# A two-level routing index, shorter last norms, reordered last sums and a gate in halves in a fused decoder layer

## What is computed

```python
x = _layernorm(x + attn(x))                # 32 heads of 8, relative bias, softmax
x = _layernorm(x + xattn(ctx_1024, x))     # state scan over 256 tokens, 16 states, gated by silu(x)
x = _layernorm(x + ffn(x))                 # 4 experts, top 1: y_e(x) * softmax weight
```

```python
logits = x @ Wr + br
probs = softmax(logits)
top_w, top_idx = top_k(probs, 1)
h = silu(x @ Wg[e]) * (x @ Wu[e]);  y = h @ Wd[e];  out = y[top_idx] * top_w
```

## Time and profile before

| what | value |
|---|---|
| median of three runs | 485.94 us |
| the profiled execution | 486.2 us |
| its span, first to last instruction | 484.5 us |
| mean granted TensorE clock | 0.958 of full speed |
| busy: PE, PEld | 427.5 us (88%), 215.6 us (45%) |
| busy: DVE, POOL, ACT | 316.5 us, 224.7 us, 210.1 us |
| DMA | 49.37 MB, mean 102 GB/s |

### The profile page before, as it was taken

How to read it: one execution, slowest core, us unless ns; L and a number is a source line. 1 busy time by engine, 2 the same in 40 slices (tenths; PEclk the granted TensorE clock), 3 DMA queues, 4 the chain that set the end, 5 groups by cost and what they waited for, 6 DMA issues and landing times.

```text
span 484.5 us, 8012 instructions
## 1 busy us (share of the span) xinstructions
PE 427.5 (88%) x2643; PEld 215.6 (45%) x2644; DVE 316.5 (65%) x620; ACT 210.1 (43%) x410; POOL 224.7 (46%) x246
## 2 busy tenths in 40 slices
PE   5889698868788998989989999876899999999993
PEld 3445123323234443444434443454446666666652
DVE  3598568999987888868888776588113334433344
ACT  2556446657554556745766458311011222111120
POOL 2000518787786679967799589300541111111001
PEclk9999766999989999999999999989799999999998
DMA  8789939527254282744345320198110000000000
GB/s 234 106 261 96 336 101 113 110 99 99 87 100 100 79 118 88 135 152 197 132 156 147 115 87 1 37 361 254 50 38 11 12 4 8 11 11 11 11 2 8
DMA packets 39366, 49.37 MB, mean 102 GB/s; under 512 B 4664, under 2 KB 32673, under 8 KB 39334
## 3 DMA queue, kind: packets, MB, share of 16 engines
q1 hardware_dynamic: 36322, 46.65, 37.8%
q0 software_dynamic: 1056, 2.10, 1.4%
q10 hardware_dynamic: 1956, 0.21, 0.4%
HBM read 40.72 MB, written 8.91 MB: 102 GB/s over the span
## 4 chain that ended last, share of the span: by engine, by line
PE 61%; DVE 20%; issue 7%; POOL 7%; ACT 2%; DMA 2%; POOLq 0%; SPq 0%; DVEq 0%
PE ps L1144 16%; PE ps L1160 8%; PE ps L870 7%; PE ps L897 5%; DVE arena L1532 5%; PE ps L901 4%; PE ps L943 4%; DVE arena L1465 4%; PE ps L770 3%; DVE arena L1483 3%; POOL arena L641 2%; PE ps L930 2%; PE ps L1152 2%; POOL arena L647 2%; PE ps L783 1%
## 5 line engine op out<-in xcount | busy, mean ns | idle before, releaser
L1336 ACT ACTIVATE arena<-ps 128x512 f32<-128x512 f32 x128 | 76.2, 595 | 90.7 <-PE ps L930 90.5
L1483 DVE TENSOR_REDUCE arena<-ps 128x2 f32<-128x512 f32 x128 | 86.3, 681 | 27.4 <-PE ps L901 23.3
L647 POOL TENSOR_TENSOR arena<-arena 128x512 f32<-128x512 f32 x60 | 76.3, 1272 | 41.6 <-DVE arena L1532 41.5
L641 POOL TENSOR_TENSOR arena<-arena 128x512 f32<-128x512 f32 x64 | 87.1, 1363 | 4.2 <-issue 4.0
L1144 PE MATMUL ps<-arena 128*128 x176 | 77.5, 593 | 0.6 <-ACT arena L1373 0.6
L1532 DVE TENSOR_TENSOR_SCAN arena<-ps,arena 128x512 f32<-128x512 f32 x60 | 72.8, 1214 | 0.5 <-DVE mv L1577 0.2
L870 PE MATMUL ps<-arena,identf 128*128 128x512 f32 x128 | 68.5, 625 | 0.0
L897 PE MATMUL ps<-arena 48*128 48x256 bf16 x256 | 52.1, 285 | 16.3 <-DVE arena L1483 11.0
L1295 ACT ACTIVATE ps<-arena 128x255 f32<-128x255 f32 x128 | 60.4, 473 | 2.4 <-DVEq L1669 2.4
L1769 DVE TENSOR_TENSOR arena<-arena,ps 128x1024 f32<-128x1024 f32 x11 | 13.4, 1220 | 64.9 <-ACT arena L1377 64.9
L717 POOL DMA_INDIRECT out<-rows_s,arena x11 | 10.8, 985 | 88.7 <-DVE rows_s L1798 80.5
(11 more groups left out here) (217 smaller groups left out, 541.3 us busy)
## 6 DMA issues: line engine op xcount, KB each, us to landing
arena<-bc_d SPq DMA_DIRECT2D x32, 512.0 KB, 4.4
arena<-in_L_ffn_Wg SPq DMA_DIRECT2D x8, 512.0 KB, 5.8
arena<-in_L_ffn_Wu SPq DMA_DIRECT2D x8, 512.0 KB, 6.3
arena<-in_L_ffn_Wd SPq DMA_DIRECT2D x4, 1024.0 KB, 12.2
arena<-kp_d SPq DMA_DIRECT2D x8, 384.0 KB, 8.0
arena<-qp_d SPq DMA_DIRECT2D x8, 384.0 KB, 10.2
qp_d<-arena SPq DMA_DIRECT2D x4, 384.0 KB, 8.6
kp_d<-arena SPq DMA_DIRECT2D x4, 384.0 KB, 8.6
```

The costliest lines, as they stand in the source:

```text
L641: g.tensor_tensor(dBu[m % 3], dtu[:, :, b * SEQ:(b + 1) * SEQ], over_k(bcr[c % BC_RING][:, m % 2, 0, :]), ALU.mult).then_inc(dbu_ready, 1)
L647: g.tensor_tensor(h, h, over_k(bcr[m // 2 % BC_RING][:, m % 2, 1, :]), ALU.mult).then_inc(hc_ready, 1)
L1336: A(prob[2 * (slot % 2) + kt][:, pr * HALF:(pr + 1) * HALF], ps[:, 2 + n % 2, :], ACT.Exp).then_inc(p_ready, 1)
L1483: v.tensor_reduce(negm[b % 2][:, qt, 2 * pair:2 * pair + 2], ps[:, bank, :].rearrange("p (h k) -> p h k", h=2), axis=AX.X, op=ALU.max).the ...
```

## The change

- The one-hot rows shrink from 1,408 to 128 places: `reached`, `nreached`, `lane` and `in_tile` split `pos` into tile and lane, `tagged` spreads the three values of a token over the 11 tiles, and one matmul for each tile of tokens (128x33) replaces 11. `e_of` is made in two instructions, behind the index, and has its own semaphore; `idx_ready` comes with the index itself. `iota16` (1,408 wide) becomes `lanes` (128).
- `scale_of` takes 10 instructions in place of 13.
- `sum_states(61)` goes ahead of `weigh`, and `sum_states(63)` goes behind tail steps 1 and 5.
- The second instruction of the last `gate` is split in halves of 256 columns; PE turns each half by itself, and `add_late` takes each tile by itself.
- The last norm of x2 moves from DVE to ACT (`bias2_ready`).
- The semaphore of the expert weights is split: the first `gate_up` waits for Wg and Wu, the first `down` for Wd.
- `keep_warm` counts change: 12, (4, 4), 14, 14, 16, 8 become 12, (1, 1, 2), 10, 14, 16, 8.

```diff
-            weigh(BATCH - 1, QUADS - 1)
-            for m in range(STATES * BATCH - 3, STATES * BATCH):
-                sum_states(m)
+            sum_states(STATES * BATCH - 3)
+            weigh(BATCH - 1, QUADS - 1)
+            sum_states(STATES * BATCH - 2)
             turns.banks = (0, 1, 2)
             pe.wait_ge(hc_vector, weighed(STATES * BATCH - 1)[1])
-            for step in (1, 5, 2, 6, 3, 7):
+            for step in (1, 5):
+                tail(BATCH - 1, step)
+            sum_states(STATES * BATCH - 1)
+            for step in (2, 6, 3, 7):
                 tail(BATCH - 1, step)
...
-            turn_back(BATCH - 1)
-            keep_warm(4, 5)
-            pe.wait_ge(taken, turns.count)
-            turn_late(BATCH - 1)
-            keep_warm(4, 5)
+            for lt in range(2):
+                pe.wait_ge(gated_ready, BATCH + lt)
+                bank = turn()
+                mixed_at.append(turns.count)
+                for k in range(KT):
+                    last = nc.tensor.transpose(ps[:, bank, k * P:(k + 1) * P], gated[:, k, lt * P:(lt + 1) * P],
+                                               identf[:, :])
+                last.then_inc(turned, 1)
+            for lt in range(2):
+                keep_warm(1, 5)
+                pe.wait_ge(taken, mixed_at[lt])
...
             for t in range(TT):
                 pe.wait_ge(hot_ready, t + 1)
-                for s in range(SLOTS):
-                    last = mm(ps[:, 7, 4 * s:4 * s + 3], onehot[t][:, s * P:(s + 1) * P], tokg[:, t, 0:3],
-                              start=(t == 0 and s == 0), stop=(t == TT - 1), skip_group_check=True)
+                last = mm(ps[:, 4, 0:3 * SLOTS], onehot[t], tagged[:, t, :, :].rearrange("p c s -> p (c s)"),
+                          start=(t == 0), stop=(t == TT - 1))
...
+            keep_warm(2, 5)
             route_late(BATCH - 1)
-            keep_warm(14, 7)
+            keep_warm(10, 7)
...
             put_late(1)
+            act.wait_ge(bias2_ready, 1)
+            for t in range(TT - 2, TT):
+                A(xres[:, t, :], xres[:, t, :], ACT.Identity, bias=nwt[:, t:t + 1],
+                  scale=rstd[:, t:t + 1]).then_inc(x2_ready, 1)
             act.wait_ge(logit_dve, 1)
...
-            keep_warm(16, 4)
-            pe.wait_ge(idx_ready, 1)
+            keep_warm(16, 5)
             pe.wait_ge(rows_in[0], 16)
             turn_rows(rows_s[:, 0, :])
-            pe.wait_ge(w_in, 16 * 20)
+            pe.wait_ge(wgu_in, 16 * 16)
+            pe.wait_ge(expert_ready, 1)
             gate_up(0, expert_of(0))
...
             def scale_of(b):
...
-                link(v.tensor_scalar_mul(vb, vb, -0.5))
-                for _ in range(3):
-                    link(v.tensor_tensor(wb, rb, rb, ALU.mult))
-                    link(v.tensor_tensor(wb, wb, vb, ALU.mult))
-                    link(v.scalar_tensor_tensor(out=rb, in0=wb, scalar=1.5, in1=rb, op0=ALU.add, op1=ALU.mult))
...
+                link(v.scalar_tensor_tensor(out=halves[:, 0, :], in0=vb, scalar=0.5, in1=halves[:, 1, :], op0=ALU.mult,
+                                            op1=ALU.mult))
+                step = wb.rearrange("p (o t) -> p o t", o=1).broadcast_to([P, 2, 2])
+                for i in range(3):
+                    link(v.scalar_tensor_tensor(out=wb, in0=halves[:, 0, :], scalar=-1.0, in1=halves[:, 1, :],
+                                                op0=ALU.mult, op1=ALU.mult))
+                    if i < 2:
+                        link(v.scalar_tensor_tensor(out=halves, in0=step, scalar=1.5, in1=halves, op0=ALU.add,
+                                                    op1=ALU.mult))
...
                 dve.wait_ge(tanh_done, b + 2)
-                v.scalar_tensor_tensor(out=gated, in0=sg, scalar=1.0, in1=gated, op0=ALU.add,
-                                       op1=ALU.mult).then_inc(gated_ready, 1)
+                for lt in range(2):
+                    cols = slice(lt * P, (lt + 1) * P)
+                    v.scalar_tensor_tensor(out=gated[:, :, cols], in0=sg[:, :, cols], scalar=1.0, in1=gated[:, :, cols],
+                                           op0=ALU.add, op1=ALU.mult).then_inc(gated_ready, 1)
...
+            def add_late(t):
+                bank = turn()
+                v.scalar_tensor_tensor(out=xres[:, t, :], in0=ps[:, bank, 0:DM], scalar=0.5, in1=xres[:, t, :],
+                                       op0=ALU.mult, op1=ALU.add).then_inc(taken, 1)
+                dve.wait_ge(taken, turns.count)
+                link(v.bn_stats(stats[:, t, :], xres[:, t, :]))
+                link(v.bn_aggr(mv[:, t, :], stats[:, t, :]))
...
+            dve.sem_inc(bias2_ready, 1)
             late_logits(BATCH - 1)
...
-            dve.wait_ge(late_pe, 4)
-            centre(BATCH - 1, x2_ready)
...
+            link(v.tensor_tensor(reached, pos.rearrange("p (t o) -> p t o", o=1).broadcast_to([P, TT, SLOTS + 1]),
+                                 thr.rearrange("p (o s) -> p o s", o=1).broadcast_to([P, TT, SLOTS + 1]), ALU.is_ge))
+            link(v.tensor_reduce(nreached, reached, axis=AX.X, op=ALU.add))
+            link(v.scalar_tensor_tensor(out=lane, in0=nreached, scalar=-float(P), in1=pos, op0=ALU.mult, op1=ALU.add))
+            link(v.tensor_tensor(in_tile, reached[:, :, 0:SLOTS], reached[:, :, 1:SLOTS + 1], ALU.subtract))
+            link(v.tensor_tensor(tagged, in_tile.rearrange("p t (o s) -> p t o s", o=1).broadcast_to([P, TT, 3, SLOTS]),
+                                 tokg.rearrange("p t (c o) -> p t c o", o=1)[:, :, 0:3, :].broadcast_to([P, TT, 3, SLOTS]),
+                                 ALU.mult))
             for t in range(TT):
-                v.tensor_scalar(onehot[t], iota16, pos[:, t:t + 1], None, ALU.is_equal).then_inc(hot_ready, 1)
-
-            link(v.tensor_scalar(e_of, tile_no, tile0[:, 1:2], None, ALU.is_ge))
-            for e in range(2, EXPERTS):
-                link(v.scalar_tensor_tensor(out=e_of, in0=tile_no, scalar=tile0[:, e:e + 1], in1=e_of,
-                                            op0=ALU.is_ge, op1=ALU.add))
-            link(v.tensor_copy(e_int, e_of))
+                v.tensor_scalar(onehot[t], lanes, lane[:, t:t + 1], None, ALU.is_equal).then_inc(hot_ready, 1)
+
             dve.wait_ge(idx_pe, 1)
...
+            v.tensor_scalar_add(idx, found[:, 0, :], float(FAR)).then_inc(idx_ready, 1)
```

More of the change, by code:

```diff
@@ L233, in decoder_layer @@
         gslot = carve(SLOTS)
-        iota16 = carve(SLOTS * P // 2, dt=F16)
+        lanes = carve(P // 2, dt=F16)
+        halves = carve(4, 2, 2)
+        reached = carve(TT * (SLOTS + 1), TT, SLOTS + 1)
+        nreached = carve(TT)
+        lane = carve(TT)
+        in_tile = carve(TT * SLOTS // 2, TT, SLOTS, dt=F16)
+        tagged = carve(TT * 3 * SLOTS // 2, TT, 3, SLOTS, dt=F16)
+        from_e = carve(SLOTS * EXPERTS, SLOTS, EXPERTS)
         assert top[0] <= stacks_top // 2
         top[0] = stacks_top // 2
-        onehot = [carve(SLOTS * P // 2, dt=F16) for _ in range(TT)]
+        onehot = [carve(P // 2, dt=F16) for _ in range(TT)]
         xrow = carve(DM)
@@ L327, in decoder_layer @@
         late_act = sem("late_act")
+        bias2_ready = sem("bias2_ready")
         idx_ready = sem("idx_ready")
+        expert_ready = sem("expert_ready")
         rows_in = [sem(f"rows_in{s}") for s in range(SLOTS)]
@@ L615, in routing_constants @@
                 pool.wait_ge(b_scores, 4 * 3 * QUADS)
-                link(g.iota(thr, pattern=[[P, TT]], base=0, channel_multiplier=0,
+                link(g.iota(thr, pattern=[[P, SLOTS + 1]], base=0, channel_multiplier=0,
                             allow_small_or_imprecise_dtypes=True))
@@ L619, in routing_constants @@
                             allow_small_or_imprecise_dtypes=True))
-                link(g.iota(iota16, pattern=[[1, SLOTS * P]], base=0, channel_multiplier=0,
+                link(g.iota(lanes, pattern=[[1, P]], base=-P, channel_multiplier=0,
                             allow_small_or_imprecise_dtypes=True))
@@ L1619, in late_logits @@
                     return
-                for t in range(2):
-                    link(v.scalar_tensor_tensor(out=lg[:, 2 * b + t, :], in0=colsum, scalar=nwt[:, 2 * b + t:2 * b + t + 1],
-                                                in1=raw[:, t, :], op0=ALU.mult, op1=ALU.add))
-                for t in range(2):
-                    link(v.scalar_tensor_tensor(out=lg[:, 2 * b + t, :], in0=lg[:, 2 * b + t, :],
-                                                scalar=rstd[:, 2 * b + t:2 * b + t + 1], in1=br_s[:, :], op0=ALU.mult,
-                                                op1=ALU.add))
+                for t in two:
+                    link(v.scalar_tensor_tensor(out=lg[:, t, :], in0=colsum, scalar=nwt[:, t:t + 1], in1=br_s[:, :],
+                                                op0=ALU.mult, op1=ALU.add))
+                dve.wait_ge(late_pe, 4)
+                for i, t in enumerate(two):
```

(29 more changed lines are left out.)

30 lines of the change are left out of this document (22 added, 8 removed).

## The result

The changed kernel takes 480.45 us (median of four runs, 480.39 to 481.29) where the kernel before took 485.81 (four runs, 485.19 to 486.09). The ratio is 0.9895, with a 95% interval from 0.9878 to 0.9913: 5.4 us less by the medians, where the forecast was 480.5. The profiled execution took 480.39 us, its span 478.6.

What follows compares the result with a forecast made beforehand. From the last scans to the first `gate_up`, DVE's chain of small instructions was taken as the bound. The terms sum to -5.4 us, from a median of 485.94 to 480.5 us; range 479.2 to 482.7.

Steps and rivals of the forecast that it cites:

- last sums, to the add to x: PE's last state sums reordered around `weigh` and the tails: `put_y` comes 1.15 us earlier, between 0 and 1.7.
- two norms: `scale_of` on DVE's chain, three instructions fewer, twice: -1.17 us, between -0.8 and -1.3.
- gate in halves: Last gate to second `scale_of`: PE's transposes start after the first half while DVE does the second; -0.5 us, 0 to -0.7.
- norm of x2 to ACT, with its semaphore: Before the expert choice, DVE loses two passes, -0.65 us, and the new semaphore costs +0.1.
- five splitting instructions: Index stage on DVE: five added linked instructions, +1.5 us, between 1.0 and 2.0.
- one-hots, gap to the index: Index stage: eight shorter one-hot instructions at 0.17 each, -2.6 us; `e_of` out of the gap behind them, -0.58.
- index to gather: `idx_ready` comes with the index instruction, 0.19 in place of 0.64 us: -0.45.
- gather and rows to `gate_up`: Ahead of the experts: 16 `keep_warm` may end at 340.3, rows land at 340.1; +0.1 us, 0 to 0.4.
- Rival 1: Before the experts: the last x2 store lands at 337 to 339 and sets the gather; 481.5 to 483.5 us, chance 0.10.
- Rival 2: Slower: the x2 store, in the full queue, lands at 344.9 and delays the gather; 489.3 us, chance 0.03.
- Rival 3: In the experts: `gate_up` begins at 1.2 GHz, 0.5 to 3 us lost; 481 to 483.5 us, chance 0.14.
- Rival 4: At the tails: reordered sums bring nothing because DVE's own steps set `put_y`; 481.6 us, chance 0.08.

Runs made afterwards that it cites:

- the repeat: The changed kernel itself, unchanged, run again as reference for two further kernels: median 480.69 us, ratio 0.9889.
- the last kernel: Changed kernel with steps trimmed off DVE's chain, first late x2 store ahead of expert weights, last between second and third Wd loads: around 479.25 us, ratio 0.9880.
- the late hand-over: Changed kernel with the slots' experts made ahead of the index again and the index handed over after the gate weights: median 481.74 us, ratio 0.9927.

## Why the prediction was right

The steps of the sum, measured from the mark, with what the undoing of each part gave back:

| step | forecast | before to after | undone alone |
|---|---|---|---|
| last sums, to the add to x | -1.15 | -1.31 | +1.31 |
| two norms | -1.17 | -1.19 | +1.19 |
| gate in halves | -0.5 | -0.48 | +0.47 |
| norm of x2 to ACT, with its semaphore | -0.55 | -0.53 | +0.54 |
| five splitting instructions | +1.5 | +1.54 | -1.54 |
| one-hots, gap to the index | -3.18 | -3.31 | +2.90 and +0.64 |
| index to gather | -0.45 | -0.46 | +0.47 |
| gather and rows to `gate_up` | +0.1 | -0.03 | |

To the gather the changes add up to -5.74 us (38.81 from the mark before, 33.07 after), and to `gate_up` to -5.77. The profiled executions differ by 5.81. The sum of the forecast was -5.4.

What is gained up to `gate_up` arrives at the end undiminished: from the first `gate_up` to the end of the span it took 137.8 us before and 137.8 after (478.6 - 340.79), and 137.7 to 137.9 in 11 of the 14 profiled executions. The other three, 139.4 to 139.6, are those in which part of the first `gate_up` ran at a granted clock of 0.50.

The undone parts give 5.98 back to the gather, 0.24 more than the whole. The surplus lies in the gap behind the one-hots: before, the experts of the slots filled it and hid the end of PE's 88 matmuls, so undoing either alone charges a part of it twice.

The mechanism of the forecast held, and five of the eight terms came out within 0.04 us. The last sums, the one-hots and the gather were off by 0.16, 0.13 and 0.13.

- **Last sums.** PE's order was what counted, as forecast, but two things were not foreseen. Tail 2 began at 312.18 (forecast 312.4), 1.20 earlier against the mark, yet `put_y` gained 1.61, not 1.15. In the kernel before, PE's step 6 had to wait for DVE's second product:

```profile
314.24 0.44 PE L978 MATMUL ps<-identf,arena 128*128 128x128 f32 x2 [0.25 <-DVE arena L1566]
```

Now that product is done in time (312.06 + 0.29), and step 6 follows step 2 at once: 0.41 more. What then took part of it back is PE's product with woT, L992, from 313.08 to 314.2: DVE waits 0.30 for it. The forecast had ended the step at `put_y` and had not asked what was late next. That the term came out within 0.16 of -1.31 is partly luck, since the two nearly cancel.
- **Norms and gate.** The rows of the old instructions priced the new ones within 0.02 us. The wider instruction (128x4) costs the same 0.16 as the one on 128x2.
- **The late logits stayed hidden** (PE's last product for them ended at 326.04, DVE took it at 326.27), and so did exp: ACT's two passes took 1.09 us and ended 1.09 before exp could start.
- **One-hots.** 0.17 each was taken from bounds of 0.08 and 0.33; measured are 0.164 from start to start and 1.40 for eight. The estimate from the Trainium skill (VectorE: DVE Perf Modes, Side-by-side: where the cycles go for N=2048 bf16), 0.20 each, lies between what the next one waits for, 0.164, and the duration of one, 0.251. The gap behind them was 0.28, not the assumed 0.35.
- **Gather and rows.** The 16 idle matmuls took 4.30 us and not the forecast 4.5, and the turn of the rows was not held up, so the +0.1 did not arise. In the repeat it was +0.6.
- **The weight semaphores** had no run of their own. The first `gate_up` waited for ACT alone, as before, so nothing speaks against the forecast of nothing.
- **The iota** was worth nothing: its time became idle time. In the run with the wide one-hots it takes 1.31 us again, the idle time is 0.61 again, and the mark is no later (302.64).
- **Rival 1, the store**, was ruled out for this kernel by the gather's releaser. The forecast landing was 334.9, measured 334.3. But the margin was 1.3 us in one execution and 0.2 in the other, so the rival was nearer than the first profile shows. The run with the store one load further back shows that the mechanism is real: there the gather waited 2.9 us.
- **Rival 2**, slower by the store, found no support: the longest landing of a late store in any of these profiles was 10.9 us, where the rival took 17.8.
- **Rival 3, the clock**, did not strike in the profile of the changed kernel: the granted clock was 0.58 of full from 338 to 340 and 1.00 from 340 on, and the first `gate_up` began at 340.79. But it is there: three profiled executions paid 1.7 to 1.8 us in the first `gate_up`, and two of them had all 16 idle matmuls. The Trainium skill (TensorE: Matmul & The Clock Gate, Part 1) has activity as what releases the clock. The traces agree: with the 16 matmuls the clock was back by 340, and without them it stayed at 0.50 until 346.
- **Rival 4**, that the sums bring nothing, is refuted by the undoing: +1.31.

The low end of the range has a small slip: the store's margin of 1.1 us caps the gain at 6.5, which gives 479.4 and not 479.2. It does not bear on the result.

## What to carry to other kernels

A chain of small linked instructions can be priced to a few hundredths of a microsecond from the rows of the instructions it already has: count them, and ask of every step that is pulled forward which engine hands over the next operand. When single parts are worth less than the scatter of whole executions, compare profiles from a common mark just ahead of the changed stage, not medians. A fixed number of filler matmuls ahead of a wait has no fixed length: here it delayed the next step by 0.5 to 0.6 us in two executions in which it ran slowly, and left a gap of 1.65 to 2.81 us in four in which it ran fast. What such a gap costs has to be read from several profiles, for only one of those four paid for it.

## What the runs showed that was not expected

**The same 16 idle matmuls took between 2.76 and 5.28 us**, by the granted clock while they ran. In the changed kernel they began at full clock, it fell during them and was back by 340, as the turn of the first rows began: 4.30 us, nothing lost. Four of the variants had much the same with 4.44 us. Run again, the changed kernel had them at half rate throughout. They kept PE busy until 340.35 and delayed the first rows' turn by 0.6:

```profile
335.07 5.28 PE L868 MATMUL ps<-hank_hi,flip 128*128 128x384 f16 x16
340.15 0.63 PE L1154 MATMUL ps<-identf,rows_s 128*128 128x128 f32 x2
```

In four variants they ran at full rate, 2.76 us, and were over 1.65 to 2.81 us before the rows came. In the last kernel the clock then fell between 338 and 339, in `gate_up`, which cost 1.7 us. In the other three (the late hand-over, the old norm, the whole gate) it did not, and `gate_up` took 7.13, even behind the longest of these gaps, here with the late hand-over:

```profile
334.59 2.76 PE L868 MATMUL ps<-hank_hi,flip 128*128 128x384 f16 x16
340.16 0.44 PE L1154 MATMUL ps<-identf,rows_s 128*128 128x128 f32 x2 [2.81 <-DMA rows_s<-x_d,arena]
341.25 7.13 PE L1167 MATMUL ps<-arena 128*128 x16 [0.65 <-ACT arena L1401]
```

With the store one load further back they ran at half rate, were over 2.08 us before the rows came, and the clock, back at full by then, fell again in `gate_up`. So the length of the gap alone does not decide whether the clock falls; what does is open here. Ten more matmuls (0.17 each at full rate) would have filled the gap in the last kernel, and delayed the rows further in the execution at half rate; that was not tried.

**The stage ahead of all changes scatters by up to 2.9 us** (the mark between 302.0 and 304.9) with the same instructions. What makes it is open; no run here was aimed at it.
